# Both halves of a value product in one place in every fourth attention unit of a MetaFormer block

## What is computed

```python
q, k = _l2norm(q), _l2norm(k)                                # per head, 24 values
attn = jnp.einsum('bhnd,bhmd->bhnm', q, k) * temperature     # 1024 x 1024 per head
attn = jax.nn.softmax(attn, axis=-1)
out = jnp.einsum('bhnm,bhmd->bhnd', attn, v)
out = out.transpose(0, 2, 1, 3).reshape(B, N, C) @ proj_w.T + proj_b
```

## Time and profile before

| | us |
|---|---|
| median of three runs | 2733.79 (2733.28 to 2739.15) |
| the profiled execution | 2741.01 |
| its span | 2739.1 |
| attention stage, about | 100 to 1656 |
| one image in the middle | 96.7 to 100.3 |

### The profile page before, as it was taken

How to read it: one execution, slowest core, us unless ns; L and a number is a source line. 1 busy time by engine, 2 the same in 40 slices (tenths; PEclk the granted TensorE clock), 3 DMA queues, 4 the chain that set the end, 5 groups by cost and what they waited for, 6 DMA issues and landing times. The chain is left out here.

```text
span 2739.1 us, 58873 instructions
## 1 busy us (share of the span) xinstructions
PE 2465.8 (90%) x18693; PEld 1295.9 (47%) x18693; DVE 1683.5 (61%) x4886; ACT 1780.7 (65%) x2228; POOL 1420.5 (52%) x1137
## 2 busy tenths in 40 slices
PE   3699999999989999989999973999999999999975
PEld 2333333333333333333333321777777777777754
DVE  6557766866766766676676655555555555555522
ACT  2487777777778777767777852555565556555542
POOL 2334435534543543543454323677777777777750
PEclk9799999999999999999999987999999999999987
DMA  4221112112112111211211243444444444444429
GB/s 91 58 51 41 50 49 58 48 42 54 51 44 60 48 49 47 58 41 45 59 48 45 77 162 128 179 155 155 177 155 162 169 155 170 160 158 174 153 79 332
DMA packets 160322, 276.49 MB, mean 101 GB/s; under 512 B 21568, under 2 KB 129584, under 8 KB 150624
## 3 DMA queue, kind: packets, MB, share of 16 engines
q1 hardware_dynamic: 141648, 245.37, 27.8%
q0 software_dynamic: 13392, 27.97, 2.8%
q10 hardware_dynamic: 5056, 0.42, 0.3%
HBM read 174.07 MB, written 49.69 MB: 82 GB/s over the span
## 5 line engine op out<-in xcount | busy, mean ns | idle before, releaser
L788 ACT ACTIVATE probs<-ps_s 128x1024 f32<-128x1024 f32 x1024 | 1011.9, 1023 | 282.6 <-PE ps_s L687 260.0
L1360 POOL TENSOR_TENSOR h_split<-h_f,h_split 128x512 f16<-128x512 f32 x444 | 550.7, 1241 | 238.3 <-ACT h_f L1337 231.0
L1333 ACT ACTIVATE h_split<-ps_h,packs 128x512 f16<-128x512 f32 x444 | 305.2, 687 | 391.1 <-PE ps_h L1287 368.8
L1287 PE MATMUL ps_h<-m_xn_t,packs 128*128 128x512 f16 x2220 | 552.4, 380 | 0.5 <-DVE m_xn_t L1422 0.5
L700 PE MATMUL ps_o<-probs,v_aug 128*32 128x512 f32 x4096 | 550.6, 610 | 0.4 <-ACT probs L788 0.4
L1054 POOL TENSOR_TENSOR inv_norm<-sumsq,minus_half 128x16 f32<-128x16 f32 x128 | 378.0, 2953 | 312.4 <-DVE sumsq L997 307.6
L1301 PE MATMUL ps_y<-packs,h_split 128*128 128x192 f16 x5328 | 511.9, 245 | 0.9 <-POOL h_split L1360 0.9
L1301 PEld LDWEIGHTS ps_y<-packs,h_split 128*128 128x128 f16 x5328 | 453.0, 97 | 105.7 <-POOL h_split L1360 1.9
L687 PE MATMUL ps_s<-stacks_odd 98*128 98x512 f16 x1024 | 301.5, 386 | 17.0 <-DMA stacks_odd<-heads 10.2
L687 PE MATMUL ps_s<-even 98*128 98x512 f16 x1024 | 299.0, 383 | 11.6 <-ACT probs L788 5.7
L1337 ACT ACTIVATE h_f<-ps_h,packs 128x512 f32<-128x512 f32 x444 | 302.0, 680 | 0.0
(11 more groups left out here) (213 smaller groups left out, 2812.6 us busy)
## 6 DMA issues: line engine op xcount, KB each, us to landing
packs<-expert_pack SPq DMA_DIRECT2D x74, 1635.0 KB, 6.6
even<-heads SPq DMA_DIRECT2D x192, 96.0 KB, 2.4
stacks_odd<-heads SPq DMA_DIRECT2D x192, 96.0 KB, 2.4
tile_rows<-sorted_rows SPq DMA_DIRECT2D x37, 400.0 KB
tokens<-in_x_dram SPq DMA_DIRECT2D x17, 768.0 KB, 5.3
y_in<-y_tokens SPq DMA_DIRECT2D x16, 768.0 KB, 8.9
out_dram<-y_out SPq DMA_DIRECT2D x16, 768.0 KB, 7.1
even<-heads SPq DMA_DIRECT2D x128, 48.0 KB
```

Of the source, the lines that this page charges most:

```text
L788: act.activation(probs[:, u % PRING, :], ps_s[:, u % 2, :, :].rearrange("p f n -> p (f n)"), ACT.Exp).then_inc(s_probs, 1)
L1287: mm = pe.matmul(ps_h[:, n % HBUF, :], w1(par, slot, w, k), xn_t[0:rows_k, par, c, :], start=(i == 0), stop=(i == 4))
L1333: act.activation(h_split[:, n % HSPLIT, 0, :], ps_h[:, n % HBUF, :], ACT.Gelu, bias=bias1(par, slot, k), scale=1.0 / WSCALE)
L1360: pool.tensor_tensor(h_split[:, n % HSPLIT, 1, :], h_f32[:, n % HBUF, :], h_split[:, n % HSPLIT, 0, :], ALU.subtract).then_inc(s_h, 1)
```

## The change

The halves stand in every fourth unit, 1, 5, 9 and so on, two at a time, f = 0 and then f = 1. In such a unit (from unit 5 on) PE first does the unit's jobs, then the scores of the next unit, then both halves. The next unit therefore starts with its jobs. The two halves that belong to the image before still stand in unit 1, behind its jobs, without the next unit's scores ahead of them; before, they stood in units 1 and 3. DVE takes the second bank one unit earlier. The jobs, their order among themselves, and what every engine computes stay as they are.

```diff
-PV_AT = range(1, UNITS, 2)
-TAKE_AT = (2, 4)
+PV_AT = range(1, UNITS, GH)
+TAKE_AT = (2, 3)
...
-            if attend:
+            if attend and not (u - 1 in PV_AT and u - 1 >= PV_LAG):
                 scores(pe, img, par, u)
-            if u in PV_AT and u >= PV_LAG and attend:
-                pv(pe, img, par, (u - PV_LAG) // 2)
-            elif u in PV_AT and u < PV_LAG and has_post(img):
-                pv(pe, img - 1, 1 - par, PVS + (u - PV_LAG) // 2)
             for job in jobs_at(img, u):
                 pe_job(pe, img, par, n, job)
                 n += 1
+
+            if u in PV_AT and u >= PV_LAG and attend:
+                scores(pe, img, par, u + 1)
+                for f in range(2):
+                    pv(pe, img, par, (u - PV_LAG) // 2 + f)
+            elif u in PV_AT and u < PV_LAG and has_post(img):
+                for f in range(2):
+                    pv(pe, img - 1, 1 - par, PVS + (u - PV_LAG) // 2 + f)
```

## The result

The changed kernel is slower. Its median is 2805.27 us (2801.93 to 2806.93, four runs), beside 2735.36 us (2733.28 to 2739.15) for the kernel before: a ratio of 1.0259, with an interval of 1.0247 to 1.0272. The forecast was 2780 us. The time lies within the range of 2732 to 2822, on the side that was forecast, and 25 us above the forecast.

A forecast was written before the change was run, and what follows sets the result against it. PE has no slack outside the middle and ACT little; in the middle, chains through DVE or ACT decide. Fourteen images 39, image 0 2.4, last image 5.5: +47 us on 2741.0 is 2788, less 7.2 for the median: 2780, range 2732 to 2822.

The forecast's parts named there:

- The walk of ACT: Quiet round of four units without jobs: 5.04 us, with ACT idle 1.26 us before the first exponential behind each pair.
- units 6 to 14: Two rounds of an image, one with x5: 10.3 us against 8.90, +1.4 us an image.
- units 46 to 62: Four rounds of an image, 6.9, 5.96 and twice 5.04 us: 23.0 against 21.68, +1.3 us an image.
- Parts costed at nothing: Takes in units 2 and 3, SP, POOL, transfers, expert and output stages, and the last image's first rounds: no cost.
- PE's saving: Two halves in one place save PE 0.19 us a pair, 49 us for 256 pairs, only where PE ends last.
- The details named for the middle: Units 18 to 46: a3 follows n4 at once; b4 waits 0.6 to 0.8 us for the copy of q4.
- ACT's wait for scores: Sign to look for: it would grow from 166.6 us in the 1000 us window by some 40 to 60 us.
- Units 62 to 6 and 14 to 18: Image borders 10.3 us against 10.34, 0.0; units 14 to 18 5.6 against 5.69, -0.1 us an image.
- Image 0: First image, without jobs of an earlier image: +2.4 us by the same walk.
- PE's saving comes through: Rival: ACT's idle time fits its slack; 2685 us if ACT never matters, about 2710 if in half the rounds; chance 0.13.
- It cancels: Rival: the middle gives back the +2.6 us lost outside it, as pairs hide waits; 2732 to 2742 us; chance 0.11.
- The middle loses too: Rival: jobs that lost their half as cover wait for DVE, +3 us an image; 2822 us; chance 0.14.

## Why the forecast was right, and where it was short

**The walk of ACT held to 0.01 us in rounds without jobs.** 5.04 us for a round was forecast, and 5.03 is measured; for ACT's idle time 1.26, and the rows show 1.26 to 1.31. Late in the last image, where the earlier trace rows had 4.17 us for four exponentials, the timeline of ACT now has:

```profile
1696.10 3.77 ACT L792 ACTIVATE probs<-ps_s 128x1024 f32<-128x1024 f32 x4 [1.31 <-PE ps_s L687]
1701.13 3.77 ACT L792 ACTIVATE probs<-ps_s 128x1024 f32<-128x1024 f32 x4 [1.26 <-PE ps_s L687]
```

That one mechanism makes up most of the loss: +1.49 us in units 6 to 14, +1.70 in units 46 to 62, and +5.3 in units 34 to 62 of the last image, where +5.5 was forecast. PE's idle time ahead of scores, 1.34 and 1.84 us in the two stretches for 0.00 and 0.15 before, and the kernels with the short exponential show that it is ACT.

**Parts costed at nothing that cost nothing** are the take, the early scores in sum, and SP, POOL and the later stages. The last image's first rounds absorbed theirs: units 22 to 34 became 3.45 us shorter, as DVE and PE stand still there anyway, while units 2 to 22 became 2.75 longer.

**PE's saving** is real only where ACT is out of the way, and then 0.13 us rather than 0.19.

**The details named for the middle** came out in part. a3 follows n4 at once, as in PE's timeline of image 6 (q1, the pair, n4, a3), so that the 2.65 us of the earlier trace rows are covered:

```profile
743.31 0.61 PE L743 MATMUL ps_m<-ident,heads 128*96 128x128 f16 x8
...
744.28 1.92 PE L700 MATMUL ps_o<-probs,v_aug 128*32 128x512 f32 x16
746.14 0.34 PE L731 MATMUL ps_m<-ident,xn_split 128*128 128x128 f16 x3
746.32 0.39 PE L749 MATMUL ps_m<-ident,o_sb 128*128 128x128 f32 x2
```

b4 came late, but its wait wasn't the one forecast: n7 ahead of it idled 0.52 us for DVE (768.97), and b4 started at 769.36, when the copy of q4 was done (768.21 + 1.02 = 769.23), where 0.6 to 0.8 us for that copy were forecast. ACT's wait for scores grew by 33 us, though, and not by 40 to 60, and as it grew by 50 in the faster kernel with single halves behind the jobs, it was no good sign to name.

**The terms that were too small** account for 17 of the 25 us; most are terms of the sum; the clock, and the start and end of the last image, stood at nothing in it.
- The clock. After a wait in the middle the granted clock falls in some images. Units 22 to 26 took 9.04 us in image 5 and 7.44 in image 4:

```profile
628.97:638.01 9.04, 7.99 (x53) 3.43 (x51) 5.41 (x17) 4.53 (x5) 7.01 (x5) 0.81 0.08 25
525.73:533.17 7.44, 6.35 (x53) 3.09 (x51) 5.43 (x17) 4.53 (x5) 5.78 (x4) 1.00 0.04 14
```

  That is 1.6 us each in images 3, 5, 8 and 13, and once in units 6 to 10 of image 11: 8 us in all. Without them units 18 to 46 would have changed by -0.4 us on average, and +0.2 was forecast.
- Units 46 to 50 took 7.43 us, with 6.9 forecast: 0.5 us x 12 images. a6 must wait for v7 to leave its bank; that was in the sum, but DVE does a step of its own before it. In DVE's timeline of image 6:

```profile
775.44 0.56 DVE L1011 TENSOR_TENSOR heads<-scale,heads 128x384 f32<-128x384 f32 x1
...
776.55 0.25 DVE L843 SCALAR_TENSOR_TENSOR heads<-ps_m,bias_qkv 128x96 f32<-128x96 f32 x1
```

  v7 starts at 774.94 on PE, its last take ends at 776.80, and a6 starts at 776.86, 1.92 us after v7.
- Units 62 to 6 and 14 to 18: +0.3 us each above their terms, 8 us in all. 5.85 us for units 14 to 18 instead of 5.6; units 2 to 6 took 4.0 us and more for the 3.6 of the walk, and the borders of the loop cost what they cost before, to within a microsecond or two.
- Image 0 cost 2.4 us more than forecast, and the last image 2.7. Image 0 was given the walk of the others though its rounds had been shorter to start with. In the last image the forecast had the late rounds right; what it left out is the way from u62 of image 14 to u2, +2.2 us, and from u62 to the end, +1.5.

These are 8 + 6 + 8 + 5 = 27 us, less what the middle without the clock gave back, 0.63 x 14, 9 us: some 18 us.

**The other 8 us are no mechanism.** The profiled execution of before, 2741.01 us, lay above all its timed runs, and the sum was made against it and then shifted down by the distance to the median. The profiled execution of after lies at its median (2804.95 and 2805.27). Against the profiles alone the forecast was +47, measured +64.

**The rivals.** PE's saving comes through: no, ACT's slack of 3.3 us for four rounds was the right ground to reject it. It cancels: no. The middle loses too: its mechanism was there, and its sum was not. From u18 to u46 jobs wait for DVE 4.99 us an image, 3.09 before, +1.9 where the rival had +3; other waits that shrank and less busy time made it good. The forecast called the middle neutral, +0.2, and +0.03 was measured. That was luck: by the experiments it is a gain from the jobs' new place, -0.9 us, and a loss from the pairs of about as much, half of that from the clock, and the forecast hadn't told them apart.

## What to carry to other kernels

Two score buffers give the consumer two units of cover. Before work is grouped on the engine that feeds it, walk one round trip: the group's length plus the restart against the consumer's time for what is buffered. Here it said 1.26 us of idle time for 0.19 us saved, in a round of 5.04 us, and 5.03 was measured. When a change moves two things, cost each alone: the part that was worth having here, the halves behind the jobs, gains 0.8% by itself, and it was buried under the other. Kept to chosen units it gained 1.0 and 1.3% in two runs; the 1.3 has the unexplained short round in it, and the 1.0 isn't told from 0.8 by these intervals. Judge a wait by what the limiting engine idles for it: the waits of ACT and of PE's weight loads grew in a kernel that got faster. And a forecast from one profiled execution should be given as a difference from that execution, and its position among the runs not be carried over as if it were a constant.

## What the runs showed of the hardware

The granted clock of PE fell to its lower level, 1.2 of 2.4 GHz, for 3.41 us at a time in images 1 to 14 of the two kernels. The trace of before has four such falls there, all at borders between images; the trace of after has seven, two at borders and five within images, and the kernel with pairs ahead of the jobs has 23. The other kernels with pairs and a full exponential have six to eight, those with single halves two to five, each by one profiled execution. Ahead of the fall in image 5 PE had waited for DVE, then ran a pair at the lower level, 3.38 us for 16 products instead of 1.92:

```profile
628.79 0.34 PE L731 MATMUL ps_m<-ident,xn_split 128*128 128x128 f16 x3 [1.34 <-DVE heads L843]
628.97 0.60 PE L687 MATMUL ps_s<-stacks_odd 98*128 98x512 f16 x2
629.49 3.38 PE L700 MATMUL ps_o<-probs,v_aug 128*32 128x512 f32 x16
```

The same wait in image 6 was 1.37 us long, at 729.98, and no fall came there. So the wait alone doesn't decide it. The kernels with pairs had more such falls.

One and the same kernel also showed a round of 6.46 us on one chip and 7.5 us on another, at the same place in images 3 to 14, with ACT and DVE both late and nothing in the profile to wait for. Such a difference is as large as many a change, so a comparison across chips is safe only for differences well above it.
